# Feed-forward of a decoder layer: second products of two pairs in a row, gelu's output in eight buffers, the next batch's transposes among the products

## The reference

```python
def _L0_ffn_ref(x, U1, V1, b1, U2, V2, b2):     # D_MODEL, D_FF, RANK = (256, 1024, 64)
    P = jnp.einsum('bsd,dr->bsr', x, U1)
    H = jax.nn.gelu(jnp.einsum('bsr,rf->bsf', P, V1) + b1)
    Q = jnp.einsum('bsf,fr->bsr', H, U2)
    return jnp.einsum('bsr,rd->bsd', Q, V2) + b2
...
x = _layernorm(x + _L0_ffn_ref(x, ...), axis=-1)
```

## Time and profile before

| | us |
|---|---|
| median of 3 runs | 2195.38 |
| lowest and highest | 2195.28, 2197.44 |
| the profiled execution, its time | 2197.36 |
| the profiled execution, its span | 2195.6 |
| `ffn` in it, from its first matmul | 1978 to 2195.6 |
| one step of `ffn` in its middle | 12.3 |

### The profile page before, as it was taken

The page is one execution under the profiler, slowest core; times in us unless marked ns, Lnnn a source line. Parts: engine busy times, 40 slices in busy tenths (PEclk is TensorE's granted clock), DMA queues, the critical chain, the costliest instruction groups (busy, mean ns, idle before and its releaser), DMA issues. The chain is left out here.

```text
span 2195.6 us, 39396 instructions
## 1 busy us (share of the span) xinstructions
PE 1985.4 (90%) x12897; PEld 1348.4 (61%) x12960; DVE 1468.2 (67%) x2652; ACT 1222.3 (56%) x2425; POOL 883.2 (40%) x1336
## 2 busy tenths in 40 slices
PE   6786949999999868999999999999999999968997
PEld 4665337888888755566566665566655665535554
DVE  6898634555555427777778777777777787724776
ACT  6775535555555423665656656565656556645554
POOL 3443615555555431334333434344333433332222
PEclk9999969999999979999999999999999999978999
DMA  3343121211122244343443344342443334112221
GB/s 116 123 149 125 44 77 68 77 68 69 67 73 76 78 106 91 77 106 72 104 105 85 79 93 103 92 103 64 109 103 80 90 81 94 43 39 66 78 87 66
DMA packets 104787, 188.10 MB, mean 86 GB/s; under 512 B 27961, under 2 KB 78137, under 8 KB 98489
## 3 DMA queue, kind: packets, MB, share of 16 engines
q1 hardware_dynamic: 104632, 186.13, 31.7%
HBM read 110.23 MB, written 58.79 MB: 77 GB/s over the span
## 5 line engine op out<-in xcount | busy, mean ns | idle before, releaser
L1516 ACT ACTIVATE at_pt<-at_ps_w 128x512 f32<-128x512 f32 x640 | 377.8, 598 | 232.8 <-PE at_ps_w L1392 232.7
L1743 DVE TENSOR_REDUCE at_mneg<-at_ps_s 128x1 f32<-128x384 f32 (+3 forms) x704 | 437.3, 636 | 94.9 <-PE at_ps_s L1381 87.3
L1606 POOL TENSOR_SCALAR_AFFINE_SELECT at_pt<-at_pt 128x256 f32<-128x256 f32 (+1 forms) x640 | 233.5, 368 | 576.3 <-ACT at_pt L1516 573.8
L1380 PE MATMUL at_ps_s<-at_ks,at_qs 96*128 96x128 bf16 (+3 forms) x1024 | 259.4, 306 | 25.0 <-DVE at_mneg L1743 22.7
L1392 PE MATMUL at_ps_w<-at_qs,at_ks 97*128 97x512 bf16 (+3 forms) x1024 | 244.3, 301 | 9.0 <-ACT at_pt L1516 5.0
L1380 PEld LDWEIGHTS at_ps_s<-at_ks,at_qs 96*128 96x128 bf16 x1024 | 86.2, 99 | 215.1 <-DVE at_mneg L1743 140.5
L895 POOL TENSOR_TENSOR ml_m_lo<-ml_m,ml_m_hi 128x512 fp32r<-128x512 f32 x80 | 115.9, 1450 | 181.0 <-ACT ml_m_hi L801 180.7
L1408 PE MATMUL at_ps_o<-at_pt,at_val 128*32 128x512 f32 (+3 forms) x2048 | 169.1, 449 | 9.7 <-POOL at_pt L1606 9.5
L1381 PE MATMUL at_ps_s<-at_mask,at_ident 128*128 128x128 bf16 (+1 forms) x641 | 149.4, 233 | 0.0
L834 ACT ACTIVATE ml_gl<-ml_ps_g 128x512 f32<-128x512 f32 x96 | 56.7, 591 | 153.8 <-PE ml_ps_u L127 150.0
L1392 PEld LDWEIGHTS at_ps_w<-at_qs,at_ks 97*128 97x128 bf16 x1024 | 88.3, 98 | 62.9 <-ACT at_pt L1516 14.8
(11 more groups left out here) (255 smaller groups left out, 5582.3 us busy)
## 6 DMA issues: line engine op xcount, KB each, us to landing
parts_d<-at_parts SPq DMA_DIRECT2D x64, 384.0 KB, 2.5
at_ks<-parts_d SPq DMA_DIRECT2D x192, 128.0 KB, 7.8
at_qs<-parts_d SPq DMA_DIRECT2D x32, 384.0 KB, 5.7
pj_xin<-in_x SPq DMA_DIRECT2D x16, 512.0 KB, 5.3
gate_d<-pj_zc SPq DMA_DIRECT2D x16, 512.0 KB, 2.7
xv_all<-pj_turned_xv SPq DMA_DIRECT2D x16, 512.0 KB, 4.2
ml_turned_y<-xv_all SPq DMA_DIRECT2D x16, 512.0 KB, 3.4
ml_x<-gate_d SPq DMA_DIRECT2D x16, 512.0 KB, 4.3
```

The source lines that it names most:

```text
L1380: pe.matmul(out[:, i, :], qs[par][0:ROWS, h, toks], ks[par][0:ROWS, h, 0:(qt + 1) * P], start=i == 0, stop=False)
L1516: act.activation(pt[u % RING][:], ps_w[u % 2][:], ACT.Exp, scale=SCALE).then_inc(exped, 1)
L1606: pool.affine_select(out=diag, in_=diag, compare_op=ALU.is_ge, fill=0.0, base=0, pattern=pattern, channel_multiplier=-1).then_inc(cut, 1)
L1743: dve.tensor_reduce(mneg[:, g, h0 % HG:h0 % HG + count, qt], view_score(ps_s[s % 2], qt, count), AX_X, ALU.max, negate=True).then_inc(maxe ...
```

## The change

- Gelu's output goes to eight buffers `hid` instead of four, so it waits for the previous batch's `second` of the same pair and for nothing of its own batch.
- TensorE runs `second` in twos: `second(b-1, 2)` with `second(b-1, 3)`, and `second(b, 0)` with `second(b, 1)`.
- On TensorE `hidden(b, 0)` stands ahead of `turn(b+1, 0)`, and `turn(b+1, 1)` ahead of `hidden(b, 1)`. Between the two transposes now stand two seconds; before, one second and four hidden tiles. `last_product(b-1)` and `first(b+1)` come one after the other.
- ScalarE runs `gelu(b, 0)` ahead of `second_high(b-1)` and `high(b+1, 1)` ahead of `gelu(b, 1)`.
- VectorE runs `first_low(b+1)` ahead of `add_x(b-1)`.

```diff
@@ ffn
         n.sb("feed", [P, (fw.end - nc.sbuf_base) // 4])
+        hid += [n.sb(f"hid{i}", [P, T]) for i in range(4, HT)]
...
-                    mm = pe.matmul(ps_q[half * RANK:(half + 1) * RANK, :], raw_u2[:, k, :], hid[k % RING][:],
+                    mm = pe.matmul(ps_q[half * RANK:(half + 1) * RANK, :], raw_u2[:, k, :], hid[k][:],
...
             def step(b, par):
                 begun = not (isinstance(b, int) and b == 0)
                 more = not is_last(b)
+                hidden(b, par, 0)
                 if more:
                     turn(b + 1, 1 - par, 0)
                 if begun:
+                    second(b - 1, 2)
                     second(b - 1, 3)
-                hidden(b, par, 0)
-                hidden(b, par, 1)
                 if more:
                     turn(b + 1, 1 - par, 1)
-                second(b, 0)
+                hidden(b, par, 1)
+                hidden(b, par, 2)
                 if begun:
                     last_product(b - 1, 1 - par)
-                hidden(b, par, 2)
-                second(b, 1)
                 if more:
                     first(b + 1, 1 - par)
+                second(b, 0)
+                second(b, 1)
                 hidden(b, par, 3)
-                second(b, 2)
             over(pe, B, step)
+            second(B - 1, 2)
             second(B - 1, 3)
...
-                    if j >= 2:
-                        act.wait_ge(q_ready, HT // 2 * b + j - 1)
-                    else:
-                        wait(act, q_ready, HT // 2 * (b - 1) + j + 3)
-                    act.activation(hid[k % RING][:], ps_h[k % RING][:], ACT.Gelu_apprx_tanh, bias=bias1[:, k:k + 1]).then_inc(gelu_done, 1)
+                    wait(act, q_ready, HT // 2 * (b - 1) + j + 1)
+                    act.activation(hid[k][:], ps_h[k % RING][:], ACT.Gelu_apprx_tanh, bias=bias1[:, k:k + 1]).then_inc(gelu_done, 1)
...
+                gelu(b, 0)
                 if not (isinstance(b, int) and b == 0):
                     second_high(b - 1, 1 - par)
-                gelu(b, 0)
-                gelu(b, 1)
                 if more:
                     high(b + 1, 1 - par, 1)
+                gelu(b, 1)
                 gelu(b, 2)
...
                 if more:
                     low(b + 1, 1 - par, 1)
-                if begun:
-                    add_x(b - 1, 1 - par)
                 if more:
                     first_low(b + 1, 1 - par)
                 if begun:
+                    add_x(b - 1, 1 - par)
                     layernorm(b - 1, 1 - par)
```

## The result

The changed kernel takes 2257.79 us (median of 4 runs, 2255.23 to 2261.4) against 2195.33 before (4 runs, 2191.24 to 2197.44). The ratio is 1.0284, with a 95% interval of 1.0262 to 1.0305: slower by some 62 us, inside the forecast range of 2226 to 2284 and 7 us under the forecast of 2265.

What follows compares the result with a forecast made beforehand. Two chains were taken to bind at once, TensorE's 12.19 us and the one over VectorE's 12.33. Terms 43.4 + 1 + 2.5 + 22.8 = +69.7 us gave 2265 us from the median 2195.38; range 2226 to 2284.

Steps and rivals of the forecast that it cites:

- Both large terms: In the 13 steps of ffn: VectorE's new order at +43.4 us and TensorE's low clock at +22.8 us.
- The order of VectorE: Middle steps: add_x behind first_low delays layernorm, low and the transposes; step 15.66 us instead of 12.33, +43.4 us.
- The clock: TensorE behind each 3.7 us pause: 3.5 us at half speed, 1.75 us a step, +22.8 us over 13 steps.
- the rival's 2242: TensorE behind the pauses: the clock stays up, 2242 us; chance 0.25 for clock up or lost in few steps.
- TensorE's own work: TensorE's instructions in a step of the changed kernel: 11.9 us against 12.19 before.
- That rival: Middle steps: TensorE stays the bound and the change brings what it saves, -6.5 us, 2189 us; chance 0.05.
- `layernorm` escapes `residual`: Rival, VectorE beside GpSimd: layernorm wins the race for the ports, step 13.58 us, about 2214 us; chance 0.11.
- Start and tail: Before the 13 intervals, little between turn(1, 0) and turn(1, 1), +1 us; at the end, second_low(14) behind delayed layernorm, +2.5.
- ScalarE's moves, SyncE's load and the eight buffers at nothing: Middle steps: moved ScalarE jobs have room, the load is not needed for 9 us more, gelu's old wait held nothing; no cost.

Runs made afterwards that it cites:

- the unused matmuls: Changed kernel with 12 matmuls a step added behind second(b-1, 3), in front of the waiting transposes, their results used by nobody: 2240.61 us, ratio 1.0209.
- `add_x` early again: Changed kernel with VectorE running add_x(b-1) ahead of first_low(b+1) again, all else as changed: 2206.82 us, ratio 1.0045.
- residual first: Changed kernel with GpSimd running residual(b+1) ahead of ln_root(b-1): 2221.45 us, ratio 1.012.
- `add_x` late alone: Kernel before with only VectorE's swap, first_low(b+1) ahead of add_x(b-1): 2289.57 us in one run.

## Why the prediction was right

The split of the measured difference in the two profiles, `ffn` alone, is +60.7 us (278.34 - 217.65), against +69.7 forecast. Both large terms had their mechanism right and were a little too large; no large errors cancelled (-4.5, -3.1, -2.6 and +1.2 us). By the steps of the prediction:

- **The order of VectorE, forecast +43.4, measured +38.9.** 15.31 us in the interval at full clock against 12.32, times 13. The mechanism is shown from three sides: swapping `add_x` back removes it, swapping it alone in the kernel before makes it, and the chain closes to the hundredth. The size was 0.35 us a step too high: 0.11 up to `add_x`, 0.08 to `residual`, 0.14 to `low`, 0.02 to the transposes. The timeline of that interval:

```profile
2004.17 0.40 PE L125 MATMUL ff_ps_t<-ff_x_hi,fw_u 128*128 128x512 f32 x1
```

```profile
2005.77 0.60 ACT L1904 ACTIVATE ff_pp<-ff_ps_t 128x512 fp32r<-128x512 f32 x1 [1.77 <-PE ff_ps_t L127]
...
2007.12 1.23 DVE L1986 TENSOR_TENSOR ff_r<-ff_ps_o,ff_xb 128x1024 f32<-128x1024 f32 x1
...
2011.59 2.34 POOL L1947 TENSOR_TENSOR ff_xb<-fw_xin,fw_bias 128x1024 f32<-128x1024 f32 x1
2011.65 3.40 DVE L1999 TENSOR_SCALAR ff_r<-ff_r,ff_mv,ff_lnr 128x256 f32<-128x256 f32 x4 [1.53 <-POOL ff_lnr L1955]
2014.97 0.68 DVE L1971 TENSOR_TENSOR ff_x_lo<-ff_ps_t,ff_x_hi 128x512 fp32r<-128x512 f32 x1
```

  From the transposes (2000.39) `first` starts at 3.78 (forecast 3.87) and `add_x` at 6.73 (6.84); `residual` follows after 4.47 (4.55) and `low` after 3.38 (3.52).
- **The clock, forecast +22.8, measured +19.7.** All 12 later intervals lost it, the first did not: its pause lay at its end. I had counted 13. An interval loses 1.64 us and not 1.75, and 12 x 1.64 = 19.7. A mean clock of 0.90 between the levels 0.5 and 1.0 is 2 x 0.10 x 16.93 = 3.4 us of the step at the low one, where I had 3.5; half of it is 1.7, and the last 0.06 stays open. The kernel with the unused matmuls, in which the clock stays up, landed at 2240.6, near the rival's 2242. The rows under this term were thinner than they looked. I wrote that pauses of up to 2.49 us did not lose the clock, but the trace of before has one of 1.60 us (857.64 to 859.24) with a mean clock of 0.53 in the 3.60 us behind it, and one of 2.66 us that lost it too (last section). That the clock fell in every step was the likelier case by my rows, and no more than that.
- **TensorE's own work, forecast 11.9, measured 11.49.** This term was 0.4 us a step too high, and it did not show in the time, as the wait hid it. Two `second`s in a row take 1.87 us, not 1.99: the pair in the earlier trace rows perhaps waited for a gelu, which in that row's step ended at 2171.79, where the latter half of the pair was due at 2171.87; no run tested that. The transposes ahead of a hidden pair take 0.41 and not 0.59, which is their price ahead of a `second`; the second matmul of the hidden pair then starts 0.32 behind the first instead of 0.23. That rival, at its right price and with the chain opened, would be some 2184 to 2187 instead of 2189.
- **`layernorm` escapes `residual`: no.** `residual` began 0.06 us ahead of it, as worked out, and `layernorm` took 3.40 us. Moved apart by hand it takes 1.38.
- **Start and tail, forecast +1 and +2.5, measured -1.6 and +3.7.** Some 1.3 of the -1.6 are luck with the clock at the start of `ffn`, as shown above, and about -0.3 is left for the change. The tail carries one more stretch at the low clock, some 1.7 us, which I had put into the 13 steps; without it, it would be +2.0.
- **ScalarE's moves, SyncE's load and the eight buffers at nothing** held: the buffers alone gave no gain in the steps, and between 2000 and 2220 no engine of the changed kernel waited for a load.

## What to carry to other kernels

Before moving an instruction on an in-order engine, follow the loop from it back to itself across a step: here `low` to transposes to `first` to `first_low` to `add_x` to `layernorm` to `low`. Putting the one that was ready early behind one that is ready late lengthens that loop by nearly the whole difference (here `add_x` starts 3.22 us later and the loop is 2.99 longer at the full clock), and an engine that is busy for only 8.94 of 16.93 us then sets the step. A pause of the matmul engine can cost more than itself, so price the clock behind it as a term of its own; and if the profile shows two chains within about 1% of each other, open the second before working on the first.

## What the runs showed of the hardware that I had not expected

- The same pause gave both answers. Behind 3.8 us the clock was low in all 12 steps of the changed kernel, behind 1.3 us (`add_x` early again) in none, but behind 2.4 us (residual first) in 3 of 12 with the same instructions ahead of it. Even the pause of 2.49 us at 838.23 in the earlier trace rows, behind which the clock stayed at 1.00, is no rule: it lies in a stage that all kernels share, and in the profile of `add_x` early again the same pause and the 3 us behind it read

```profile
841.18:843.68 2.50, 0.00 (x1) 0.01 (x1) 1.28 (x3) 1.67 (x4) 0.00 (x0) 1.00 0.46 157
843.68:846.68 3.00, 3.00 (x17) 2.11 (x18) 2.54 (x6) 1.33 (x3) 1.16 (x1) 0.66 0.23 80
```

  and in the kernel before a pause of 2.66 us lost the clock:

```profile
58.05:60.71 2.66, 0.00 (x1) 0.01 (x1) 2.44 (x4) 1.76 (x5) 0.93 (x2) 1.00 0.81 319
60.71:64.10 3.39, 3.39 (x12) 3.09 (x13) 1.50 (x2) 0.61 (x1) 1.20 (x1) 0.50 0.72 214
```

  A pause in that region has no single price; what decides it was not tried.
- The clock need not fall in the pause. Timeline of TensorE in the changed kernel, one restart:

```profile
2168.67 0.48 PE L1843 MATMUL ff_ps_h<-ff_pp,fw_v 128*128 128x512 f32 x1
2168.99 0.40 PE L1844 MATMUL ff_ps_h<-ff_pp,fw_v 128*128 128x512 f32 x1
2169.22 0.53 PE L1843 MATMUL ff_ps_h<-ff_pp,fw_v 128*128 128x512 f32 x1
2169.55 0.63 PE L1844 MATMUL ff_ps_h<-ff_pp,fw_v 128*128 128x512 f32 x1
2169.97 0.63 PE L1843 MATMUL ff_ps_h<-ff_pp,fw_v 128*128 128x512 f32 x1
```

  The transposes and the first two matmuls run at 2.4 GHz (the second and third start 0.23 apart), and from the fourth on they run at 1.2 (0.42 apart). Over the 12 slow steps the fall comes later each time, from under 0.1 to 1.4 us after TensorE began again, and the steps cost the same (16.91 to 17.03 us).
- In the kernel with `add_x` late alone the steps alternate, near 18.25 and 19.27 us. The clock alternates with them. Two steps of it, each from its later transposes on:

```profile
2059.13:2064.40 5.27, 5.27 (x19) 3.33 (x20) 1.23 (x2) 0.60 (x1) 0.00 (x0) 0.50 0.64 199
2064.50:2078.00 13.50, 9.43 (x41) 4.94 (x39) 7.31 (x15) 6.69 (x11) 3.52 (x3) 1.00 0.00 0
```

```profile
2078.40:2081.50 3.10, 3.10 (x9) 1.16 (x9) 1.23 (x2) 0.60 (x1) 0.00 (x0) 0.50 0.82 259
2081.50:2095.10 13.60, 10.71 (x50) 6.22 (x50) 6.15 (x12) 6.69 (x11) 3.52 (x3) 1.00 0.04 18
```

  After its restart TensorE runs for 2.2 us longer at the low level in the longer step, and half of that is the 1 us between the two. Why the clock alternates was not tried.
- The stages ahead of `ffn`, the same code in every kernel, end up to 10 us apart from run to run, and TensorE's clock at the start of `ffn` moves its length by 1 to 2 us more. A change of one stage is told better by the length of its steps than by the time of the launch.
